# Second layer's context attention: shift-row DMAs on SyncE, exponents over two steps, division moved, values' bias in the output's

## The reference, cut

```
x = x + _L1_xattn_ref(_layernorm(x), ctx_1024, ctx_1024, Wq, bq, Wk, bk, Wv, bv, Wo, bo)

q = query @ Wq.T + bq;  k = key @ Wk.T + bk;  v = value @ Wv.T + bv      # split in 16 heads
scores = einsum('bhtd,bhsd->bhts', q, k) / sqrt(32)
attn = softmax(scores, axis=-1)
ctx = einsum('bhts,bhsd->bhtd', attn, v)
return ctx @ Wo.T + bo
```

## Time and profile before

| | us |
|---|---|
| median of 3 runs | 3909.35 |
| the three runs | 3906.99 to 3917.72 |
| the profiled execution | 3923.12 |
| its span, first to last instruction | 3921.2 |
| mean granted TensorE clock of the span | 0.986 |
| busy over the span: PE / DVE / ACT / POOL | 3746.8 / 2212.4 / 1525.4 / 1012.3 |

### The profile page before, as it was taken

How to read it: one execution, slowest core, us unless ns; L and a number is a source line. 1 busy time by engine, 2 the same in 40 slices (tenths; PEclk the granted TensorE clock), 3 DMA queues, 4 the chain that set the end, 5 groups by cost and what they waited for, 6 DMA issues and landing times. The chain is left out here.

```text
span 3921.2 us, 73601 instructions
## 1 busy us (share of the span) xinstructions
PE 3746.8 (96%) x29918; PEld 2714.0 (69%) x29918; DVE 2212.4 (56%) x4864; ACT 1525.4 (39%) x3725; POOL 1012.3 (26%) x857
## 2 busy tenths in 40 slices
PE   8999999999999999999999999999999999999897
PEld 4777777777777777867756556666666666667785
DVE  4555555555555545535555413676676766766557
ACT  3233222232323323224433222555555555565444
POOL 2020201011010202002221021354554554553222
PEclk9999999999999999999999999999999999999999
DMA  4112222212121212120040574212212212101100
GB/s 151 61 59 65 65 65 65 65 55 72 48 65 44 80 42 85 54 71 23 24 134 28 169 263 127 63 20 66 65 24 66 63 26 64 52 20 31 37 2 23
DMA packets 159837, 254.81 MB, mean 65 GB/s; under 512 B 28112, under 2 KB 66640, under 8 KB 157712
## 3 DMA queue, kind: packets, MB, share of 16 engines
q1 hardware_dynamic: 121872, 188.15, 15.2%
q0 software_dynamic: 13104, 47.98, 3.7%
q10 hardware_dynamic: 24528, 13.96, 1.7%
HBM read 216.97 MB, written 33.10 MB: 64 GB/s over the span
## 5 line engine op out<-in xcount | busy, mean ns | idle before, releaser
L581 PE MATMUL swishmax_attended<-swishmax_weights_t,swishmax_context 128*128 128x128 f32 x4096 | 520.1, 275 | 3.4 <-DVE swishmax_values_t L505 3.4
L1561 POOL TENSOR_TENSOR context_partial<-context_partial,context_weights_t 128x512 f32<-128x512 f32 x300 | 382.4, 1275 | 466.4 <-ACT context_weights_t L1589 449.9
L435 ACT ACTIVATE swishmax_xes<-swishmax_score,swishmax_neg_max 128x512 f32<-128x512 f32 x256 | 177.1, 694 | 806.9 <-DVE swishmax_neg_max L470 806.9
L581 PEld LDWEIGHTS swishmax_attended<-swishmax_weights_t,swishmax_context 128*128 128x128 f32 x4096 | 487.9, 192 | 3.8 <-issue 3.8
L1770 PE MATMUL context_bank<-ahead_stream,ahead_staged 128*128 128x512 f32 x1024 | 485.3, 617 | 3.1 <-PEq L1138 1.7
L595 PE MATMUL swishmax_bank<-ahead_stream,ahead_w 128*128 128x512 f32 x1024 | 464.2, 596 | 7.4 <-DMA ahead_stream<-in_context_t_dram 7.4
L581 PE MATMUL swishmax_attended<-swishmax_weights_t,swishmax_sides 128*128 128x128 f32 x3072 | 384.9, 275 | 0.0
L581 PEld LDWEIGHTS swishmax_attended<-swishmax_weights_t,swishmax_sides 128*128 128x128 f32 x3072 | 363.6, 192 | 0.0
L1770 PEld LDWEIGHTS context_bank<-ahead_stream,ahead_staged 128*128 128x128 f32 x1024 | 189.0, 195 | 213.4 <-issue 199.0
L1779 PEld LDWEIGHTS context_bank<-ahead_w,ahead_stream 128*128 128x128 f32 x2304 | 276.9, 192 | 80.6 <-issue 55.3
L1670 DVE TENSOR_TENSOR context_weights_t<-context_weights_t,context_spread 128x512 f32<-128x512 f32 x512 | 314.7, 679 | 30.1 <-ACT context_spread L1585 25.9
(11 more groups left out here) (379 smaller groups left out, 5787.3 us busy)
## 6 DMA issues: line engine op xcount, KB each, us to landing
ahead_stream<-in_context_t_dram SPq DMA_DIRECT2D x78, 1024.0 KB, 6.1
swishmax_context<-in_context_dram POOLq DMA_DIRECT2D x32, 1024.0 KB, 5.7
swishmax_down<-_L_xattn_value_down_dram SPq DMA_DIRECT2D x64, 256.0 KB, 4.3
swishmax_up<-in_L_xattn_value_up_dram SPq DMA_DIRECT2D x32, 512.0 KB, 5.9
ahead_values<-ahead_staged SPq DMA_DIRECT2D x14, 1024.0 KB, 8.8
context_values<-ahead_values SPq DMA_DIRECT2D x56, 256.0 KB, 3.2
experts_w<-in_L_ffn_W_dram SPq DMA_DIRECT2D x16, 512.0 KB, 12.4
context_shift<-context_minima ACTq DMA_DIRECT2D x32, 256.0 KB, 4.8
```

The lines of the kernel that those rows point to most:

```text
L435: nc.scalar.activation(xes[:, n % XES, r, :], score[r][:], ACT.Exp, bias=neg_max[:, e, r, c:c + 1]).then_inc(exped, 1)
L581: last = nc.tensor.matmul(product(i)[:, m, :], side(left, c, k, m), weights_t[:, n % 2, right, k, :], start=c == 0 and k == 0 and m == 0 a ...
L1561: link(nc.gpsimd.tensor_tensor(acc, acc, w_t[:, :, k, :], ALU.add))
```

## The change

- "minima_out" and "minima_in" go from ACT's list to SP's: `send_minima(u)` in step c = 3 (n = 4u + 3), behind SP's loads of that step. It waits for `minima_set`, issues the write, waits for `minima_landed`, issues the read-back.
- ACT: the exponents r = 0 and 1 of tile n - 5 stand at the end of step n, and r = 2 and 3 of tile n - 6 behind the copies (and behind "spread", where there is one). Key and value are evicted in between.
- DVE: "heads" stands first in step c = 2 and is two instructions long; maxima come before shifts in every step; "minima" stands behind the first two shifts.
- Values' bias: no longer added per unit. Once, in step n = 1, PE multiplies a tile that holds the bias in every column by wo ("bias", four matmuls), and DVE adds the result to `bias_o`. Four DVE instructions at the start fill that tile.

```diff
--- before.py
+++ after.py
@@ -1396,7 +1396,7 @@
...
         partial = s.sb("partial", [P, 2, HG, P])
-        inverse, quotient = s.sb("inverse", [P, P]), s.sb("quotient", [P, P])
+        inverse = s.sb("inverse", [P, P])
         queries_t = s.sb("queries_t", [P, 2, NG, P])
...
@@ -1454,28 +1454,25 @@
...
             out = [("score_t", u, c)] * (u < NU) + [("sums", u - 2)] * (c == 2 and u >= 2 and u - 2 not in TALLIED)
-            out += [("key", u + 1, c)] * (u + 1 < NU) + value_tiles(n) + [("turned", u)] * (c == NCH - 1 and u < NU)
+            out += [("key", u + 1, c)] * (u + 1 < NU) + value_tiles(n) + [("turned", u)] * (c == NCH - 1 and u < NU) + [("bias", 0)] * (n == 1)
             out += [("attend", (n - LAG) // NCH, (n - LAG) % NCH)] * (0 <= n - LAG < NU * NCH)
...
             u, c = divmod(n, NCH)
-            exps = [("exp", *divmod(n - NCH - 1, NCH), r) for r in range(HG)] * (0 <= n - NCH - 1 < NU * NCH)
-            minima = [(what, u - 1) for what in ("minima_out", "minima_in")] * (c == 0 and 1 <= u <= NU)
-            out = [("copy", u, c, r) for r in range(HG)] * (u < NU) + minima[:1] + [("spread", u - 1)] * (c == 1 and 1 <= u <= NU)
-            values = value_tiles(n)
-            out += [("key", u + 1, c)] * (u + 1 < NU) + values[:len(values) - 1]
-            return out + exps[:2] + minima[1:] + values[-1:] + exps[2:]
+            def exps(m, some):
+                return [("exp", *divmod(m, NCH), r) for r in some] * (0 <= m < NU * NCH)
+
+            out = [("copy", u, c, r) for r in range(HG)] * (u < NU) + [("spread", u - 1)] * (c == 1 and 1 <= u <= NU) + exps(n - LAG, range(2, HG))
+            return out + [("key", u + 1, c)] * (u + 1 < NU) + value_tiles(n) + exps(n - NCH - 1, range(2))
 
...
             b, g = divmod(u, NG)
-            maxima = [("max", u, c)] * (u < NU) + [("fold", u)] * (c == NCH - 1 and u < NU)
+            out = [("heads", u - 2)] * (c == 2 and u >= 2) + [("max", u, c)] * (u < NU) + [("fold", u)] * (c == NCH - 1 and u < NU)
             shifts = [("shift", *divmod(n - NCH - 1, NCH), r) for r in range(HG)] * (0 <= n - NCH - 1 < NU * NCH)
-            heads = [("heads", u - 2)] * (c == 2 and u >= 2)
-            out = maxima + shifts if c == NCH - 1 else shifts + heads + maxima if c == 0 or c == 2 else maxima + shifts
-            out += [("minima", u)] * (c == NCH - 1 and u < NU)
+            out += shifts[:2] + [("minima", u)] * (c == NCH - 1 and u < NU) + shifts[2:] + [("bias", 0)] * (n == 1)
             out += [("join", k) for k in range(2 * n + 1, min(2 * n + 3, B))] + [("stats", 0)] * (n == 3)
...
@@ -1515,6 +1512,15 @@
...
 
+                def send_minima(u):
+                    sp.wait_ge(minima_set, u + 1)
+                    sp.dma_start(minima_dram[u].rearrange("r q -> q r"), row_min[:], allow_slow_non_contiguous=True).then_inc(minima_landed, 16)
+                    sp.wait_ge(minima_landed, 16 * (u + 1))
+                    if u:
+                        sp.wait_ge(shift_spread, u)
+                    sp.dma_start(shift[:].rearrange("p r q -> p (r q)"),
+                                 broadcast(minima_dram[u].rearrange("r q -> (r q)"))).then_inc(shift_landed, 16)
+
                 def load_context(b, c):
...
@@ -1530,6 +1536,8 @@
...
                         load_context(b, c)
+                    if n % NCH == NCH - 1 and n > 0:
+                        send_minima(n // NCH)
                 for c, name in enumerate("qkvo"):
...
@@ -1587,15 +1595,6 @@
...
                         nc.scalar.activation(weights_t[:, n % SLOTS, r], weights_t[:, n % SLOTS, r], ACT.Exp).then_inc(exped, 1)
-                    elif what == "minima_out":
-                        act.wait_ge(minima_set, u + 1)
-                        act.dma_start(minima_dram[u].rearrange("r q -> q r"), row_min[:], allow_slow_non_contiguous=True).then_inc(minima_landed, 16)
-                    elif what == "minima_in":
-                        act.wait_ge(minima_landed, 16 * (u + 1))
-                        if u:
-                            act.wait_ge(shift_spread, u)
-                        act.dma_start(shift[:].rearrange("p r q -> p (r q)"),
-                                      broadcast(minima_dram[u].rearrange("r q -> (r q)"))).then_inc(shift_landed, 16)
                     elif what == "key":
...
@@ -1624,6 +1623,9 @@
...
                 first(nc.vector.memset(ones[:], 1.0))
+                for g in range(NG):
+                    last = nc.vector.tensor_scalar(heads_t[:, 1, g, :], ones[:], bias[:, 2, g:g + 1], None, ALU.mult)
+                first(last)
                 first(nc.vector.tensor_scalar(bias_q[:], bias[:, 0, :], SCALE, None, ALU.mult))
...
@@ -1674,8 +1676,7 @@
...
                         link(nc.vector.reciprocal(inverse[:], attended[:, 1]))
-                        link(nc.vector.tensor_tensor(quotient[:], attended[:, 0], inverse[:], ALU.mult))
-                        nc.vector.tensor_scalar(heads_t[:, b % 2, g, :], quotient[:], bias[:, 2, g:g + 1], None, ALU.add).then_inc(heads_out, 1)
+                        nc.vector.tensor_tensor(heads_t[:, b % 2, g, :], attended[:, 0], inverse[:], ALU.mult).then_inc(heads_out, 1)
                     elif what == "later":
...
@@ -1697,6 +1698,8 @@
...
                                                                   op0=ALU.mult, op1=ALU.add)
+                        elif what == "bias":
+                            last = nc.vector.tensor_tensor(bias_o[:], bias_o[:], ring.bank(t)[:], ALU.add)
                         elif what == "output":
...
@@ -1793,6 +1796,10 @@
...
                                                         start=c == 0, stop=c == DC - 1)
+                    elif what == "bias":
+                        pe.wait_ge(w_loaded["o"], 16)
+                        for g in range(NG):
+                            last = nc.tensor.matmul(bank_t[:], heads_t[:, 1, g, :], w["o"][:, g, :], start=g == 0, stop=g == NG - 1)
                     elif what == "output":
...
```

## The result

The changed kernel takes 3948.57 us (median of 4, 3944.32 to 3950.28), the kernel before 3908.80 us (median of 4, 3906.99 to 3917.72): ratio 1.0096, 95 % interval 1.0078 to 1.0113. It is slower by 1.0 %. The forecast was 3935 us, with a range of 3885 to 3980; "slower" had a chance of 0.54.

A forecast was written before the change was run, and what follows sets the result against it. The prediction took a loop over DMA to bound the units of the second layer's context attention. Its terms, -11 + 3 + 1.5 - 1 + 34 = +26 us, gave 3949 profiled and 3935 us as median, range 3885 to 3980.

The forecast's parts named there:

- The bound: Second layer's context attention: a loop over DMA, 36.1 us, sets the unit, not PE's own list of 31.0 us.
- The new loop: Plain unit after the change, "turned" to "turned" through both DMAs, spread, late exponents, POOL and "sums": 35.4 us.
- the DMAs' term: Shift row's write and read-back, from the write's issue to the spread copy: 13.5 us, bounds 13 and 16.
- By batch: Four units of a batch take 147.6 us against 149.2: -1.6 per batch, -11 us for seven.
- The clock: PE's granted clock falls once in each unit but the query's: 23 x 1.5 = +34 us, bounds 0 and 50.
- Division first, two instructions: DVE's "heads" in step 3 loses one instruction: priced at nothing, 36 us if "heads" were late everywhere.
- The bias: Values' bias put once into the output's, with fills, matmuls and an addition: +1.5 us, between 0 and 3.7.
- Tail: Kernel's end: last row of minima leaves earlier, held exponents wait for the spread: -1 us, within 3 either way.
- From the sum to the median: Sum of +26 us gives 3949 profiled; the 14 us lower median is carried over, giving 3935 us.
- Clock holds: Rival, chance 0.20: idle pieces on PE lower the granted clock no more often than now; 3901 us, about even.
- the write is quick from SP: Rival, chance 0.10: the 10 us belong to ACT's queue, SP's takes 2 to 4 us; 3773 us.
- DMAs as slow as now on average: Rival, chance 0.12: write to spread stays at 14.9 us, 43 us more: 3978 us.

The follow-up runs named there:

- the swap of order: Changed kernel with the two late exponents ahead of the spread copy in ACT's list, not behind it: 3842.25 us, ratio 0.9784 to the kernel before.
- The half filler: Changed kernel with 11 unused 128x128 matmuls on PE ahead of the wait of "sums": 3944.85 us, ratio 1.0049 to the kernel before.
- the two fastest kernels: Changed kernel with ACT's exponents in their old places, 3809.33 us; the same with the shift row written in 16-byte pieces, 3784.26 us.

## Why the prediction was right, point by point

**The bound.** That a loop over DMA, and not PE's list, sets the unit held: with the DMAs sent earlier no wait for POOL is left at "sums", and without the split and with a short write the unit falls to PE's list, 30.9 us. Two things were missed. PE's waits were read as small ones spread over many places, but "hidden" waited for ACT 24.8 us at 7 places, up to 5.2 at once. And in plain units the next limit lay close: with the DMAs on SP alone they fell by 0.9 us only, since "heads" and the maxima were then late.

**The new loop.** The row it rests on (exponents behind the spread) is confirmed by the swap of order. The table above sets its terms beside the unit shown; less the 1.7 us that the key's eight matmuls lost at half clock, the last of them is 13.2 us, as in the sum. The stage's mean for the two DMAs is 13.77. So the DMAs' term is 0.3 us a unit too low. The two stalls: at "sums" 3.2 us was forecast; that is the longest, and the mean is 78.5 / 30 = 2.6; at attend 1.3 was forecast, and the mean is 41.8 / 26 = 1.6.

**By batch.** 147.6 us plus the clock's 23 x 1.5 / 7 = 4.9 is 152.5; measured 151.8. By kind of unit the forecast holds too: for the plain ones it gives 37.6 on average with the clock (two of 35.4 and one of 37.6 in a batch, and 1.5 each), and 37.3 were measured; for the one with a query 39.2, and 40.1 were measured.

**The clock.** Forecast was one fall per unit but the query's, 23 in all, +34 us. Counted in the trace's record of the granted clock between 2400 and 3660 us, there are 23 low stretches after and 14 before, 106 us against 58. That the count is exactly 23 is partly luck: four plain units have none, one has two, one of the units with a query has one, and the same kernel had 26 in its second trace. The step that failed here is that the sum charged all 23 as new, where the kernel before had 14 of its own: the 48 us more at half level are worth about 24 us of full-speed work, where the sum had 34. The half filler gave the price of a fall as 1.4 us. The granted clock of the stage was forecast as 0.93 and measured as 0.96; the 0.93 didn't follow from the sum, whose 34 us are 68 us at half level, or a clock of 0.97 over the stage's 1,250 us.

**Division first, two instructions.** Priced at nothing, with 36 us as the other end and only if "heads" were late. The run with this part alone gained 16 us, bias included. The step that failed is "what waits for heads": the maxima behind it on DVE, and through them the score of c = 3, wait too. The sum did count on scores that aren't late in the changed kernel, so at least a part of this gain is contained in its -11; how much isn't shown.

**The bias.** +1.5 us, between 0 and 3.7. The tile costs 3.60, and the cover that I named, the 3.88 us wait four steps later, is there unchanged behind it. It is a wait for DVE, whose work there starts only behind PE's "turned" of that unit, so it moved along with PE and covers nothing. The upper end was the right one. The other 2.0 us ahead of the two scores lie before the first score (2427.41 before, 2429.39 after); in the twelve traces of this case that score starts between 2425 and 2437 us, so they say nothing about the change.

**Tail.** 2.4 us for all behind the 28 units; the sum had -1 for the tail and 3 for the left-over units, together +2.

**From the sum to the median.** The sum of +26 us on the profiled execution gives 3949, and 3949.72 was measured; the median forecast was 3935, and 3948.57 was measured. Of the final number the step that failed is the last one: the profiled execution of before lay 14 us above its median, and I carried this over to a kernel whose profiled execution lies 1 us above its own. By medians the change costs 40 us, by profiled executions 27. Which of the two is the better measure of before isn't settled by the first comparison; in the later sets its median was 3928 to 3929, and the ratio was the same 1.0095. The profiled sum was the better forecast, in part by luck, because its errors cancel: the clock 10 too high, the DMAs 0.3 x 28 = 8 too low, the bias 2 too low.

**The rivals.** "Clock holds" and "the write is quick from SP" fell by the traces of after: 23 low stretches, and 9.4 us from write to read-back on SP. "DMAs as slow as now on average" fell too: from write to spread they took 13.77 us on average, and 14.20 in the changed kernel's second trace, not 14.9. But the same write took 1.4 us once its pieces were 16 bytes, so the 10 us belong to the form of the transfer, and neither to ACT's queue nor to SP's. The 2 us that the prediction set beside them are, by the Trainium skill's own account (DMA: Bandwidth & Descriptors, Anatomy of one DMA), a fit for DMAs issued by GpSimd; this write is issued by ACT or SP, so the trace neither bears it out nor speaks against it.

## What to carry to other kernels

When an instruction is moved on an in-order engine, look at the wait it lands behind, and at who waits for the moved one: two exponents of 0.57 us, put behind a copy that waits for a DMA, cost 4 % of the kernel and hid a gain of 3 %. When an instruction gets shorter, ask also who waits for what is queued behind it. A round trip through DRAM is worth a look at its pieces before it is worth a reordering. And a mean over unlike units can hide changes of opposite sign: compare plain units with plain ones.

## What the runs showed of the hardware

- The same 2 KB written to DRAM in 4-byte pieces (528 packets) took 9.0 to 10.0 us on average until the next DMA was issued (means of ten traces, single ones 7.8 to 11.9), from ACT's queue as from SP's; in 16-byte pieces (144 packets) it took 1.4 us in most units, up to 5.3. In both forms the packets of the one write looked at had all started within 4 us of its issue.
- The copy of 128x512 f32 that reads its source with a step of four elements took 1.14 us on ACT, where the contiguous one takes 0.59.
- A tensor_scalar of 128x128 f32 on DVE took 0.74 to 1.35 us in the 29 units where a POOL addition ran at the same time, and 0.29 us in the three where none did (kernel before, L1678).
- In the changed kernel PE had 20 idle pieces of 3.2 us ahead of "sums". Behind 16 of them the key's eight matmuls ran slow; in the unit shown they took 5.40 us at the 1.2 GHz level instead of 3.70. Shorter pieces did it too: with 2.1 us (the 16-byte write) these matmuls were slow behind 16 of 22. The kernel before, whose pieces ahead of "sums" are 0.5 us or less, still had 14 low stretches in the stage, five of them where "hidden" waited. With "sums" waiting for nothing there were 9 (DMAs alone on SP), 2 and 1 (the two fastest kernels).
